# A mixture of experts: the 32 spare rows of each expert taken four experts at a time

## The chip, the cores and the metric

One core of a Trainium2 chip runs the whole program. The metric is the time of one execution on the device, in microseconds. Each kernel is run several times and the median counts.

## The reference

Four blocks in a row on 4096 tokens of 256 features, in fp32: attention, a local-attention transformer, a state-space scan, and a mixture of experts. The change lies in the last one. It has 32 experts; each token goes to the expert with the highest probability, and an expert takes at most 160 tokens (C below), the first ones in token order:

```python
C = int(math.ceil(CAPACITY_FACTOR * T / E))
...
g = jnp.einsum('ech,ehf->ecf', buf, w_gate)
u = jnp.einsum('ech,ehf->ecf', buf, w_up)
y = jnp.einsum('ecf,efh->ech', jax.nn.silu(g) * u, w_down)
out_tok = y.reshape(E * C, H)[jnp.clip(slot, 0, E * C - 1)]
out_tok = jnp.where(accepted[:, None], out_tok * gate[:, None], 0.0)
return (xt + out_tok).reshape(B, S, H)
```

T is 4096, E is 32, so C is 160: a tile of 128 rows and 32 spare rows. Feature sizes H and F are 256 each.

## The kernel before

Each block is one or two phases that follow one another; nothing of a phase overlaps the next, apart from early loads. The last, phase_moe, has two parts. In the first, eight chunks of 512 tokens are projected, normalised and routed; GpSimd scatters each token's row (its normalised features, its residual sum, its gate and its number: 514 fp32 words) to its expert's slot in a table in HBM, slots_x.

In the second part, here called the expert stage, the experts are taken in order, and each engine runs its own list of steps; they meet by semaphores:

- SP: load_weights(e) loads the three 256x256 matrices of expert e into a ring of RING buffers, and waits for the down products of the expert that had the buffer.
- ScalarE: load_rows(e) loads the expert's 160 rows from slots_x as two transfers (128 rows, L2852, and 32 rows, L2853). Six experts are loaded ahead of the loop; in the loop ScalarE computes the silu of expert e (L2880) and then issues the rows of expert e + 6.
- TensorE, in each turn e of its loop: expand(e), the gate and up products with the weights stationary and all 160 rows moving (L2945); turn_rows(e + 2), the transposes of the rows, for each half of the features one of 128 rows (L2932) and one of 32 (L2933); and reduce(e - 1), the down products with the rows stationary, once for 128 rows and once for 32 (L2956).
- VectorE: multiply (L2794, silu times up), put_xeT (L2786, the transposed rows out of PSUM), put_y (L2803, gate times product plus residual sum, once for 128 rows and once for 32) and tokens (L2813, the rows' numbers as integers).
- GpSimd: two indirect scatters per expert into the output (L2701).

PSUM tiles of the stage (p_x, p_g, p_u, p_y) have two buffers each, xeT and hidden two, y four and xe eight.

## Time and profile before

| what | us |
|---|---|
| median of three runs | 3643.21 |
| lowest and highest | 3635.83, 3643.5 |
| span of the profiled execution, first to last instruction | 3631.7 |

The profile is of one execution. It records the span; what lies around the span is not in it, and no time of that execution other than the span is given. All positions below are microseconds from the start of the span. Engines: PE is TensorE (PEld its weight loads), DVE is VectorE, ACT is ScalarE, POOL is GpSimd; a q behind the name is the engine's queue of DMA issues. L2945 is line 2945 of the kernel. A row of the timeline gathers neighbouring instructions of a kind: start, length, count (x8); PE's ends are modelled and overlap the next start, so a pace is read from one start to the next. An fp32 product is recorded as two instructions, a transpose as one.

### The profile page before, as it was taken

How to read it: one execution, taken by the hardware profiler on the slowest of the kernel's cores; microseconds unless marked ns; L12 is line 12 of the kernel's file. 1: busy time of each engine (PE TensorE's matmuls, PEld its weight loads, DVE VectorE, ACT ScalarE, POOL GpSimd, SP SyncE). 2: the span in 40 equal slices, each digit the busy share in tenths (PEclk: the TensorE clock that was granted, in tenths of full speed). 3: DMA queues.
4: the chain of work that ended last, by engine and by line, in shares of the span. 5: the costliest groups of instructions: out<-in, count | busy, mean ns of one | idle time of the engine just before them, and what ended most of it. 6: DMA issues, size and time to landing. Idle time of an engine off the chain costs nothing. (4 is left out here: it accounts for less than half of the span.)

```text
span 3631.7 us, 52306 instructions
## 1 busy us (share of the span) xinstructions
PE 3234.2 (89%) x18096; PEld 1975.7 (54%) x18096; DVE 2456.1 (68%) x4653; ACT 1848.7 (51%) x3942; POOL 1431.3 (39%) x992
## 2 busy tenths in 40 slices
PE   8599999979999799999999899897388888887798
PEld 5244444346666555566666555332255565555676
DVE  8488887657777522377777232598599999996633
ACT  2177776836666411266666111366377777774100
POOL 4201111132222211132222111244699999995533
PEclk9699999989999899999999899998699999999899
DMA  5945676110020133000200221343615151512873
GB/s 169 161 62 88 78 99 123 28 38 23 23 65 23 51 133 96 22 23 25 67 23 17 69 69 39 101 159 130 240 59 204 58 204 59 203 58 98 296 226 117
DMA packets 276675, 347.29 MB, mean 96 GB/s; under 512 B 71168, under 2 KB 208368, under 8 KB 275772
## 3 DMA queue, kind: packets, MB, share of 16 engines
q1 hardware_dynamic: 261860, 308.29, 30.9%
q10 hardware_dynamic: 9432, 23.35, 1.9%
q0 software_dynamic: 5120, 12.30, 0.9%
q8 instruction: 145, 2.38, 0.3%
q14 instruction: 118, 0.97, 0.1%
HBM read 227.72 MB, written 112.80 MB: 94 GB/s over the span
## 5 line engine op out<-in xcount | busy, mean ns | idle before, releaser
L2373 POOL TENSOR_TENSOR H_feed<-H_ndu,H_bs 128x1024 f32<-128x1024 f32 x256 | 595.3, 2373 | 6.3 <-DMA H_bs<-between_bc 3.2
L888 ACT ACTIVATE B_probs<-B_p_exp,B_key_bias 128x512 f32<-128x512 f32 (+3 forms) x768 | 395.0, 582 | 162.6 <-PE B_p_exp L950 132.2
L779 DVE TENSOR_REDUCE B_part_max<-B_p_max 128x1 f32<-128x512 f32 (+3 forms) x768 | 374.5, 545 | 81.9 <-PE B_p_max L914 79.4
L1298 ACT ACTIVATE D_probs<-D_scores,D_neg,D_rq 128x256 f32<-128x256 f32 x512 | 283.1, 573 | 255.6 <-DVE D_neg L1219 255.6
L2344 ACT ACTIVATE H_decay<-H_ndt,H_rate 128x1024 f32<-128x1024 f32 x256 | 287.8, 1125 | 198.0 <-DVE H_turning L2426 103.2
L1658 PE MATMUL E_p_ag<-E_hT,FA_w 128*128 128x512 f32 x640 | 283.1, 602 | 1.9 <-ACT E_hT L1614 1.9
L911 PE MATMUL B_p_max<-B_k,B_q 100*128 100x512 bf16 (+3 forms) x768 | 256.9, 341 | 29.9 <-DMA B_q<-in_q_rows 20.0
L947 PE MATMUL B_p_exp<-B_q,B_k 100*128 100x512 bf16 (+3 forms) x768 | 250.6, 330 | 23.9 <-DMA B_q<-B_shift_rows 17.1
L2426 DVE TENSOR_TENSOR_SCAN H_turning<-H_decay,H_feed 128x1024 f32<-128x1024 f32 x112 | 253.5, 2274 | 24.1 <-POOL H_feed L2373 22.7
L2477 PEld LDWEIGHTS H_p_y<-H_minus,H_sT 128*128 128x128 f32 x1792 | 224.3, 199 | 76.2 <-ACT H_sT L2329 56.1
L2477 PE MATMUL H_p_y<-H_minus,H_sT 128*128 128x128 f32 x1792 | 232.6, 286 | 35.5 <-ACT H_sT L2329 35.5
L1156 POOL TENSOR_TENSOR D_rnorm<-D_norm,D_power 128x8 f32<-128x8 f32 x64 | 106.1, 1658 | 375.0 <-DVE D_norm L1174 375.0
L1630 ACT ACTIVATE E_gated<-E_p_ag,FA_b 128x512 f32<-128x512 f32 x96 | 62.6, 652 | 372.9 <-PE E_p_ag L1658 353.7
L2329 ACT ACTIVATE H_sT<-H_p_T,H_cT 128x128 f32<-128x128 f32 x896 | 242.9, 387 | 11.7 <-PE H_p_T L2467 11.4
L1353 PE MATMUL D_p_qk<-LA_wqkv,D_hT 128*128 128x512 f32 x512 | 242.3, 617 | 0.9 <-ACT D_hT L1273 0.9
L1216 DVE CUSTOM_DVE_ANT_0 D_scores<-D_scores,D_mask 128x256 f32<-128x256 f32 x512 | 201.9, 457 | 55.0 <-PE D_scores L1380 54.8
L2426 DVE TENSOR_TENSOR_SCAN H_decay<-H_decay,H_feed 128x1024 f32<-128x1024 f32 x96 | 218.9, 2280 | 15.5 <-POOL H_feed L2373 15.5
L1160 POOL TENSOR_TENSOR D_rnorm<-D_norm,D_power 128x8 f32<-128x8 f32 x64 | 106.7, 1667 | 287.7 <-DVE D_norm L1174 287.7
L1658 PEld LDWEIGHTS E_p_ag<-E_hT,FA_w 128*128 128x128 f32 x640 | 121.9, 192 | 155.3 <-issue 151.6
L1585 DVE SCALAR_TENSOR_TENSOR E_act_out<-E_p_ag,FA_b,E_gated 128x512 f32<-128x512 f32 x96 | 67.8, 706 | 198.7 <-ACT E_gated L1630 198.7
L2485 PE MATMUL H_p_y<-H_part,H_minus 128*128 128x512 f32 x384 | 184.5, 603 | 9.6 <-DVE H_part L2402 9.5
L911 PEld LDWEIGHTS B_p_max<-B_k,B_q 100*128 100x128 bf16 x768 | 75.3, 98 | 208.2 <-DVE B_part_max L779 131.4
(269 smaller groups left out, 6858.2 us busy)
## 6 DMA issues: line engine op xcount, KB each, us to landing
H_bs<-between_bc SPq DMA_DIRECT2D x64, 512.0 KB, 8.0
H_cs<-between_bc SPq DMA_DIRECT2D x36, 512.0 KB, 8.5
B_q<-between_q_parts SPq DMA_DIRECT2D x90, 128.0 KB
B_k<-between_k_parts SPq DMA_DIRECT2D x90, 128.0 KB
between_slots_x<-E_clear ACTq DMA_DIRECT2D x4, 2570.0 KB, 18.8
I_xe<-between_slots_x ACTq DMA_DIRECT2D x32, 257.0 KB, 3.9
LA_base<-between_z SPq DMA_DIRECT2D x64, 128.0 KB, 2.2
between_z<-D_z SPq DMA_DIRECT2D x64, 128.0 KB, 1.7
```

Of the source, the lines that this page charges most:

```text
L779: nc.vector.reduce_max(part_max[:, g % 2, kc, qb, h:h + 1], p_max[:, use % 3, 0:keys], AX.X).then_inc(maxed, 1)
L888: nc.scalar.activation(probs[:, x % PROBS, skip:512], p_exp[:, n % SCORES, skip:512], ACT.Exp, bias=key_bias[:, g % SETS, kb - 4 * Q + 4, ...
L911: last = nc.tensor.matmul(p_max[:, use % 3, 0:keys], q[0:KR, u, h, qb * P:(qb + 1) * P], k[0:KR, u, h, 512 * kc:512 * kc + keys], start=Tr ...
L947: last = nc.tensor.matmul(p_exp[:, n % SCORES, skip:512], k[0:KR, u, h, kb * P:(kb + 1) * P], q[0:KR, u, h, 512 * Q + skip:512 * Q + 512], ...
L1298: last = nc.scalar.activation(probs[:, place[m], :, :].rearrange("p a b -> p (a b)"), scores[:, place[m], :, :].rearrange("p a b -> p (a b ...
L1353: last = nc.tensor.matmul(p_qk[:, m, :], hT[:, i % 2, k, :], wqkv[:, k, m * INNER:(m + 1) * INNER], start=k == 0, stop=k == KD - 1)
L1658: last = nc.tensor.matmul(p_ag[:, m % 2, n, :], w1[:, k, at:at + P], hT[:, i % 2, k, :], **flags)
L2329: last = nc.scalar.activation(sT[:, k % 2, h * HB + b, :], p_T[:, h, b, :], ACT.Copy, scale=cT[:, i % 2, h * HB + b, s:s + 1])
L2344: nc.scalar.activation(decay[:, n % 2, :], ndt[:, g % 2, :], ACT.Exp, scale=rate[:, m, s:s + 1]).then_inc(decayed, 1)
L2373: nc.gpsimd.tensor_tensor(feed[:, n % AHEAD, :], ndu[:, g % 2, :], bs[:, s, :], ALU.mult).then_inc(fed, 1)
L2426: nc.vector.tensor_tensor_scan(out, decay[:, n % 2, :], feed[:, n % AHEAD, :], 0.0, ALU.mult, ALU.add).then_inc(scanned, 1)
L2477: last = nc.tensor.matmul(p_y[:, h, b * P:(b + 1) * P], sT[:, k % 2, h * HB + b, :], minus[:, :], start=False, stop=False)
```

## The change

The expert stage treats the spare rows of four experts, a quad, as one tile of 128 rows.

- ScalarE loads an expert's 128 rows as one transfer, and the 32 spare rows of each expert of a quad into a quarter of the partitions of a tile xr, of which there are two (load_rests: four transfers). The first quad's are issued before all other rows, the second's after the first six experts' rows, and quad f + 1's in turn 4f + 1, behind the row load of that turn.
- TensorE turns the spare rows of a quad with two transposes of 128 rows, at the head of turn_rows of the quad's first expert. expand is as before, on 160 columns. reduce has only the 128 rows. Behind the reduce of a quad's last expert, reduce_rests computes the down products of the four experts' spare rows, each expert in its own strip of 32 columns of the array and its own 32 partitions of one PSUM tile.
- VectorE copies the turned spare rows once per quad and evacuates their products once per quad; GpSimd scatters them once per quad.
- xeT and hidden have eight buffers, and the ring of weights has twelve. A weight buffer is free when reduce_rests of its quad is done. p_y's two buffers are used in turn by reduce and reduce_rests.

The core of the diff:

```diff
-        K, XB, RING, XE, YR = CHUNKS, 4, 10, 8, 4
+        K, XB, RING, XE, YR = CHUNKS, 4, 12, 8, 4
+        QUAD, HR = 4, 8
+        QUADS = EXPERTS // QUAD
...
-        token_int = a.sb("token_int", [P, XE, 2, 1], I32)
+        token_int = a.sb("token_int", [P, XE, 1], I32)
+        token_rest = a.sb("token_rest", [P, 2, 1], I32)
...
-        xe = a.sb("xe", [P, XE, 2, ROW])
-        xeT = a.sb("xeT", [P, 2, KD, CAPACITY])
+        xe = a.sb("xe", [P, XE, ROW])
+        xr = a.sb("xr", [P, 2, ROW])
+        xeT = a.sb("xeT", [P, HR, KD, CAPACITY])
         sg = a.sb("sg", [P, 2, KD, CAPACITY])
-        hidden = a.sb("hidden", [P, 2, KD, CAPACITY])
-        y = a.sb("y", [P, YR, 2, DIM])
+        hidden = a.sb("hidden", [P, HR, KD, CAPACITY])
+        y = a.sb("y", [P, YR, DIM])
+        y_rest = a.sb("y_rest", [P, 2, DIM])
...
-        p_x = bank[:, 0:2, 0:KD * CAPACITY]
+        p_x = bank[:, 0:2, 0:KD * P]
+        p_xr = bank[:, 0, KD * P:2 * KD * P].rearrange("p (k j n) -> p k j n", k=KD, j=QUAD)
         p_g = bank[:, 2:4, 0:KD * CAPACITY]
         p_u = bank[:, 4:6, 0:KD * CAPACITY]
-        p_y = bank[:, 6:8, :].rearrange("p u (s d) -> p u s d", s=2)
+        p_y = bank[:, 6:8, 0:DIM]
...
+        def y_use(e):
+
+            return e + e // QUAD
+
+        def rest_use(f):
+            return f * (QUAD + 1) + QUAD
...
             def load_weights(e):
                 r = e % RING
-                reached(sp, down, e - RING + 1)
+                if e >= RING:
+                    sp.wait_ge(down, e - RING + 1)
+                    sp.wait_ge(rest_down, (e - RING) // QUAD + 1)
                 for dst, name in ((wg, "w_gate"), (wu, "w_up"), (wd, "w_down")):
...
             for e in range(EXPERTS):
-                pool.wait_ge(y_ready, e + 1)
+                pool.wait_ge(y_ready, y_use(e) + 1)
                 pool.wait_ge(tokens_ready, e + 1)
-                for t, rows in enumerate((P, REST)):
-                    pool.indirect_dma_start(T["out"][:, :], bass.IndirectOffsetOnAxis(token_int[0:rows, e % XE, t, :], axis=0),
-                                            y[0:rows, e % YR, t, :], None, bounds_check=TOKENS - 1, oob_is_err=False
-                                            ).then_inc(returned[e % YR], 16)
+                pool.indirect_dma_start(T["out"][:, :], bass.IndirectOffsetOnAxis(token_int[:, e % XE, :], axis=0),
+                                        y[:, e % YR, :], None, bounds_check=TOKENS - 1, oob_is_err=False
+                                        ).then_inc(returned[e % YR], 16)
+                if e % QUAD == QUAD - 1:
+                    f = e // QUAD
+                    pool.wait_ge(y_ready, rest_use(f) + 1)
+                    pool.wait_ge(rest_tokens_ready, f + 1)
+                    pool.indirect_dma_start(T["out"][:, :], bass.IndirectOffsetOnAxis(token_rest[:, f % 2, :], axis=0),
+                                            y_rest[:, f % 2, :], None, bounds_check=TOKENS - 1, oob_is_err=False
+                                            ).then_inc(rest_returned[f % 2], 16)
...
             def put_xeT(e):
                 dve.wait_ge(xe_turned, e + 1)
-                reached(dve, gate_up, 2 * (e - 1))
-                nc.vector.tensor_copy(xeT[:, e % 2, :, :].rearrange("p k n -> p (k n)"), p_x[:, e % 2, :]
+                reached(dve, gate_up, 2 * (e - HR + QUAD if e % QUAD == 0 else e - HR + 1))
+                if e % QUAD == 0:
+                    own = slice(e % HR, e % HR + QUAD)
+                    nc.vector.tensor_copy(xeT[:, own, :, P:CAPACITY], p_xr.rearrange("p k j n -> p j k n"))
+                nc.vector.tensor_copy(xeT[:, e % HR, :, 0:P], p_x[:, e % 2, :].rearrange("p (k n) -> p k n", k=KD)
                                       ).then_inc(xeT_ready, 1)
 
             def multiply(e):
                 u = e % 2
                 dve.wait_ge(silu, e + 1)
                 dve.wait_ge(gate_up, 2 * e + 2)
-                reached(dve, down, e - 1)
-                nc.vector.tensor_tensor(hidden[:, u, :, :].rearrange("p k n -> p (k n)"),
+                if e >= HR:
+                    dve.wait_ge(down, e - HR + 1)
+                    dve.wait_ge(rest_down, (e - HR) // QUAD + 1)
+                nc.vector.tensor_tensor(hidden[:, e % HR, :, :].rearrange("p k n -> p (k n)"),
                                         sg[:, u, :, :].rearrange("p k n -> p (k n)"), p_u[:, u, :], ALU.mult
                                         ).then_inc(hidden_ready, 1)
 
...
+                reached(dve, returned[b], 16 * (e // YR))
+                nc.vector.scalar_tensor_tensor(y[:, b, :], p_y[:, y_use(e) % 2, :], xe[:, x, GATE:GATE + 1], xe[:, x, SUM],
+                                               ALU.mult, ALU.add).then_inc(y_ready, 1)
+
+            def put_y_rest(f):
+                dve.wait_ge(rest_down, f + 1)
+                reached(dve, rest_returned[f % 2], 16 * (f // 2))
+                nc.vector.scalar_tensor_tensor(y_rest[:, f % 2, :], p_y[:, rest_use(f) % 2, :], xr[:, f % 2, GATE:GATE + 1],
+                                               xr[:, f % 2, SUM], ALU.mult, ALU.add).then_inc(y_ready, 1)
...
                     put_xeT(e + 2)
                 if e:
                     put_y(e - 1)
+                    if e % QUAD == 0:
+                        put_y_rest(e // QUAD - 1)
                 tokens(e)
+                if e % QUAD == 1:
+                    tokens_rest(e // QUAD)
             put_y(EXPERTS - 1)
+            put_y_rest(QUADS - 1)
...
             def load_rows(e):
                 b, at = e % XE, e * CAPACITY
                 reached(act, xe_turned, e - XE + 1)
-                reached(act, y_ready, e - XE + 1)
+                if e >= XE:
+                    act.wait_ge(y_ready, y_use(e - XE) + 1)
                 reached(act, tokens_ready, e - XE + 1)
-                act.dma_start(xe[:, b, 0, :], T["slots_x"][at:at + P, :]).then_inc(xe_loaded[b], 16)
-                act.dma_start(xe[0:REST, b, 1, :], T["slots_x"][at + P:at + CAPACITY, :]).then_inc(xe_loaded[b], 16)
+                act.dma_start(xe[:, b, :], T["slots_x"][at:at + P, :]).then_inc(xe_loaded[b], 16)
+
+            def load_rests(f):
+                if f >= 2:
+                    act.wait_ge(xe_turned, (f - 2) * QUAD + 1)
+                    act.wait_ge(y_ready, rest_use(f - 2) + 1)
+                    act.wait_ge(rest_tokens_ready, f - 1)
+                for j in range(QUAD):
+                    at = (f * QUAD + j) * CAPACITY + P
+                    act.dma_start(xr[REST * j:REST * j + REST, f % 2, :], T["slots_x"][at:at + REST, :]
+                                  ).then_inc(xr_loaded[f % 2], 16)
...
+            load_rests(0)
             for e in range(XE - 2):
                 load_rows(e)
+            load_rests(1)
...
                 if e + XE - 2 < EXPERTS:
                     load_rows(e + XE - 2)
+                if e % QUAD == 1 and QUAD <= e < EXPERTS - QUAD:
+                    load_rests(e // QUAD + 1)
...
             def turn_rows(e):
-                b, u = e % XE, e % 2
-                pe.wait_ge(xe_loaded[b], 32 * (e // XE + 1))
+                b, u, f = e % XE, e % 2, e // QUAD
+                pe.wait_ge(xe_loaded[b], 16 * (e // XE + 1))
                 reached(pe, xeT_ready, e - 1)
+                if e % QUAD == 0:
+                    pe.wait_ge(xr_loaded[f % 2], 16 * QUAD * (f // 2 + 1))
+                    for k in range(KD):
+                        nc.tensor.transpose(p_xr[:, k, :, :].rearrange("p j n -> p (j n)"),
+                                            xr[:, f % 2, k * P:(k + 1) * P], ident[:, :])
                 for k in range(KD):
-                    cols = slice(k * P, (k + 1) * P)
-                    at = k * CAPACITY
-                    nc.tensor.transpose(p_x[:, u, at:at + P], xe[:, b, 0, cols], ident[:, :])
-                    last = nc.tensor.transpose(p_x[:, u, at + P:at + CAPACITY], xe[0:REST, b, 1, cols],
-                                               ident[0:REST, 0:REST])
+                    last = nc.tensor.transpose(p_x[:, u, k * P:(k + 1) * P], xe[:, b, k * P:(k + 1) * P], ident[:, :])
                 last.then_inc(xe_turned, 1)
...
+                                                    ww[:, r, k, m * P:(m + 1) * P], xeT[:, e % HR, k, :],
...
             def reduce(e):
-                r, u = e % RING, e % 2
+                r, u = e % RING, y_use(e) % 2
                 pe.wait_ge(hidden_ready, e + 1)
-                reached(pe, y_ready, e - 1)
-                for t, rows in enumerate((P, REST)):
-                    for k in range(KD):
-                        last = nc.tensor.matmul(p_y[0:rows, u, t, :], hidden[:, u, k, t * P:t * P + rows],
-                                                wd[:, r, k, :], start=k == 0, stop=k == KD - 1)
+                reached(pe, y_ready, y_use(e) - 1)
+                for k in range(KD):
+                    last = nc.tensor.matmul(p_y[:, u, :], hidden[:, e % HR, k, 0:P], wd[:, r, k, :],
+                                            start=k == 0, stop=k == KD - 1)
                 last.then_inc(down, 1)
+
+            def reduce_rests(f):
+                u = rest_use(f) % 2
+                pe.wait_ge(y_ready, rest_use(f) - 1)
+                for k in range(KD):
+                    for j in range(QUAD):
+                        e = f * QUAD + j
+                        last = nc.tensor.matmul(p_y[REST * j:REST * j + REST, u, :], hidden[:, e % HR, k, P:CAPACITY],
+                                                wd[:, e % RING, k, :], start=k == 0, stop=k == KD - 1,
+                                                tile_position=(0, REST * j))
+                last.then_inc(rest_down, 1)
...
                 if e:
                     reduce(e - 1)
+                    if e % QUAD == 0:
+                        reduce_rests(e // QUAD - 1)
             reduce(EXPERTS - 1)
+            reduce_rests(QUADS - 1)
```

Two places of the program, as the engines' lists have them. TensorE before, one turn of the loop: down products, expand, four transposes, down products of the next:

```order
L2956 MATMUL I_bank<-I_wd,I_hidden 128x256 x2
L2956 MATMUL I_bank<-I_wd,I_hidden 32x256 x2
L2945 MATMUL I_bank<-I_xeT,I_wg 128x160 x4
L2945 MATMUL I_bank<-I_xeT,I_wu 128x160 x4
L2932 MATMUL I_bank<-I_ident,I_xe 128x128
L2933 MATMUL I_bank<-I_ident,I_xe 128x32
L2932 MATMUL I_bank<-I_ident,I_xe 128x128
L2933 MATMUL I_bank<-I_ident,I_xe 128x32
```

TensorE of the change, from the end of turn 4 through turn 5 to the transposes of turn 6 (L3014 is reduce, L3024 reduce_rests, L3004 expand, L2990 and L2993 turn_rows):

```order
L3014 MATMUL I_bank<-I_wd,I_hidden 128x256 x2
L3024 MATMUL I_bank<-I_wd,I_hidden 32x256 x8
L3004 MATMUL I_bank<-I_xeT,I_wg 128x160 x4
L3004 MATMUL I_bank<-I_xeT,I_wu 128x160 x4
L2993 MATMUL I_bank<-I_ident,I_xe 128x128 x2
L3014 MATMUL I_bank<-I_wd,I_hidden 128x256 x2
L3004 MATMUL I_bank<-I_xeT,I_wg 128x160 x4
L3004 MATMUL I_bank<-I_xeT,I_wu 128x160 x4
L2990 MATMUL I_bank<-I_ident,I_xr 128x128 x2
L2993 MATMUL I_bank<-I_ident,I_xe 128x128 x2
```

The 32-row products have left reduce and stand once per quad, and the quad's transposes (of xr) stand one turn behind the turn in which ScalarE issues their loads, as the next lists show. ScalarE before, one turn (silu, two row loads) and the head of the next:

```order
L2880 ACTIVATE I_sg<-I_bank 128x320
L2852 DMA I_xe<-between_slots_x 128x514
L2853 DMA I_xe<-between_slots_x 32x514
L2880 ACTIVATE I_sg<-I_bank 128x320
L2852 DMA I_xe<-between_slots_x 128x514
```

ScalarE of the change, turns 4, 5 and 6 (L2936 is the silu, L2897 load_rows, L2906 load_rests):

```order
L2936 ACTIVATE I_sg<-I_bank 128x320
L2897 DMA I_xe<-between_slots_x 128x514
L2936 ACTIVATE I_sg<-I_bank 128x320
L2897 DMA I_xe<-between_slots_x 128x514
L2906 DMA I_xr<-between_slots_x 32x514 x4
L2936 ACTIVATE I_sg<-I_bank 128x320
```

The second transfer of each expert has gone, and in turn 5 four stand between its row load and the silu of turn 6.

## Rows read from the trace of the kernel before

**Rows 1.** The page's head: length of the profiled execution.

```profile
span 3631.7 us, 52306 instructions
```

**Rows 2.** Chain that ended last, 3400 to 3632 us: shares, then start, length.

```profile
by line: PE I_bank L2945 33.5%; PE I_bank L2956 28.0%; PE I_bank L2932 5.1%; PE I_bank L2933 4.7%; PE I_bank L2892 4.7%; POOL between_slots_x L2679 4.3%; issue 4.2%; DMA between_slots_x<-I_row,I_slot_int 2.5%; DMA I_xe<-between_slots_x 1.7%
...
3403.82 0.87 PE I_bank L2901 x8
3407.76 7.00 PE I_bank L2892 x32
...
3440.14 5.91 DMA between_slots_x<-I_row,I_slot_int
...
3447.48 4.06 DMA I_xe<-between_slots_x
...
3452.95 4.21 PE I_bank L2945 x16
```

**Rows 3.** Timeline of TensorE, one expert: start, length, engine, line, what.

```profile
3534.76 1.35 PE L2945 MATMUL I_bank<-I_xeT,I_wg 128*128 128x160 f32 x8
...
3537.04 0.27 PE L2932 MATMUL I_bank<-I_ident,I_xe 128*128 128x128 f32 x1
...
3537.85 2.11 PE L2956 MATMUL I_bank<-I_wd,I_hidden 128*128 128x256 f32 x8
3539.89 1.35 PE L2945 MATMUL I_bank<-I_xeT,I_wg 128*128 128x160 f32 x8
```

**Rows 4.** Timeline of TensorE, the last experts.

```profile
3611.98 1.25 PE L2945 MATMUL I_bank<-I_xeT,I_wu 128*128 128x160 f32 x8
3613.07 1.03 PE L2956 MATMUL I_bank<-I_wd,I_hidden 128*128 128x256 f32 x4
```

**Rows 5.** Timeline of TensorE, attention and feed-forward: products in column strips.

```profile
427.10 0.64 PE L965 MATMUL B_p_acc<-B_probs,B_v 128*32 128x256 f32 x8
427.68 0.28 PE L911 MATMUL B_p_max<-B_k,B_q 100*128 100x256 bf16 x1
...
1284.46 1.95 PE L1663 MATMUL E_p_ag<-E_hT,FA_w 128*64 128x256 f32 x16
1286.34 1.09 PE L1644 MATMUL E_p_T<-FA_ident,E_hn 128*128 128x128 f32 x8
```

**Rows 6.** Timeline of all engines: SP's and ScalarE's DMA issues in one expert.

```profile
3534.86 0.37 SPq L2638 DMA_DIRECT2D I_wg<-in_w_gate  x1
...
3536.15 0.44 ACT L2880 ACTIVATE I_sg<-I_bank 128x320 f32<-128x320 f32 x1 [4.69 <-PE I_bank L2945]
3536.23 0.33 ACTq L2852 DMA_DIRECT2D I_xe<-between_slots_x  x1
...
3536.59 0.45 ACTq L2853 DMA_DIRECT2D I_xe<-between_slots_x  x1
```

**Rows 7.** DMA issues, 3480 to 3560 us: count, KB, median us to landing.

```profile
I_xe<-between_slots_x ACTq DMA_DIRECT2D x16, 257.0 KB, 3.9
...
I_xe<-between_slots_x ACTq DMA_DIRECT2D x16, 64.2 KB, 4.8
```

**Rows 8.** DMA issues, 3426 to 3440 us, the burst before the stage.

```profile
I_wd<-in_w_down SPq DMA_DIRECT2D x4, 256.0 KB, 7.7
...
between_slots_x<-I_row,I_slot_int POOLq DMA_INDIRECT x7, 6.3
```

**Rows 9.** Timeline of TensorE behind a gap (in brackets, with its releaser).

```profile
2472.12 1.13 PE L2131 MATMUL F_p_dt<-F_low,F_w_dt 16*128 16x512 f32 x4 [2.22 <-ACT F_low L2012]
```

**Rows 10.** Windows: length, PE, PEld, DVE, ACT, POOL busy; PEclk, DMA, GB/s.

```profile
2474.00:2477.00 3.00, 3.00 (x5) 1.13 (x4) 3.00 (x2) 2.03 (x4) 2.67 (x1) 0.50 0.01 1
...
3472.00:3552.00 80.00, 80.00 (x439) 58.10 (x438) 30.45 (x94) 7.00 (x16) 28.03 (x32) 1.00 0.79 242
```

**Rows 11.** Timeline of all engines at the end.

```profile
3617.16 0.86 DVE L2803 SCALAR_TENSOR_TENSOR I_y<-I_bank,I_xe 128x256 f32<-128x256 f32 x2 [1.06 <-PE I_bank L2956]
...
3620.54 0.88 POOL L2701 DMA_INDIRECT out_x<-I_y,I_token_int  x1 [0.30 <-issue]
```

More of the change, by code:

```diff
@@ L2604, in phase_moe @@
         xe_loaded = [a.sem(f"xe_loaded_{b}") for b in range(XE)]
+        xr_loaded = [a.sem(f"xr_loaded_{b}") for b in range(2)]
         xe_turned = a.sem("xe_turned")
@@ L2610, in phase_moe @@
         down = a.sem("down")
+        rest_down = a.sem("rest_down")
         y_ready = a.sem("y_ready")
@@ L2613, in phase_moe @@
         tokens_ready = a.sem("tokens_ready")
+        rest_tokens_ready = a.sem("rest_tokens_ready")
         returned = [a.sem(f"returned_{b}") for b in range(YR)]
+        rest_returned = [a.sem(f"rest_returned_{b}") for b in range(2)]
         block = ctx.enter_context(nc.Block())
@@ L2697, in _ @@
             for e in range(EXPERTS):
-                pool.wait_ge(y_ready, e + 1)
+                pool.wait_ge(y_ready, y_use(e) + 1)
                 pool.wait_ge(tokens_ready, e + 1)
-                for t, rows in enumerate((P, REST)):
-                    pool.indirect_dma_start(T["out"][:, :], bass.IndirectOffsetOnAxis(token_int[0:rows, e % XE, t, :], axis=0),
-                                            y[0:rows, e % YR, t, :], None, bounds_check=TOKENS - 1, oob_is_err=False
-                                            ).then_inc(returned[e % YR], 16)
+                pool.indirect_dma_start(T["out"][:, :], bass.IndirectOffsetOnAxis(token_int[:, e % XE, :], axis=0),
[8 more added lines that the diff above has]
+                                            ).then_inc(rest_returned[f % 2], 16)
             for b in range(YR):
-                pool.wait_ge(returned[b], 32 * EXPERTS // YR)
+                pool.wait_ge(returned[b], 16 * EXPERTS // YR)
+            for b in range(2):
+                pool.wait_ge(rest_returned[b], 16 * QUADS // 2)
         @block.vector
@@ L2798, in put_y @@
             def put_y(e):
-                u, b, x = e % 2, e % YR, e % XE
+                b, x = e % YR, e % XE
                 dve.wait_ge(down, e + 1)
-                reached(dve, returned[b], 32 * (e // YR))
-                for t, rows in enumerate((P, REST)):
-                    last = nc.vector.scalar_tensor_tensor(y[0:rows, b, t, :], p_y[0:rows, u, t, :],
-                                                          xe[0:rows, x, t, GATE:GATE + 1], xe[0:rows, x, t, SUM],
-                                                          ALU.mult, ALU.add)
@@ L2806, in put_y @@
-                last.then_inc(y_ready, 1)
+                reached(dve, returned[b], 16 * (e // YR))
[6 more added lines that the diff above has]
+                                               xr[:, f % 2, SUM], ALU.mult, ALU.add).then_inc(y_ready, 1)
@@ L2808, in tokens @@
             def tokens(e):
                 x = e % XE
-                dve.wait_ge(xe_loaded[x], 32 * (e // XE + 1))
-                reached(dve, returned[e % YR], 32 * (e // YR))
-                for t, rows in enumerate((P, REST)):
-                    last = nc.vector.tensor_scalar(token_int[0:rows, x, t, :], xe[0:rows, x, t, TOKEN:TOKEN + 1],
-                                                   -1.0, float(TOKENS), ALU.mult, ALU.add)
-                last.then_inc(tokens_ready, 1)
+                dve.wait_ge(xe_loaded[x], 16 * (e // XE + 1))
@@ new lines, in tokens, with tokens_rest @@
+                reached(dve, returned[e % YR], 16 * (e // YR))
+                nc.vector.tensor_scalar(token_int[:, x, :], xe[:, x, TOKEN:TOKEN + 1], -1.0, float(TOKENS), ALU.mult, ALU.add
+                                        ).then_inc(tokens_ready, 1)
+            def tokens_rest(f):
+                dve.wait_ge(xr_loaded[f % 2], 16 * QUAD * (f // 2 + 1))
+                reached(dve, rest_returned[f % 2], 16 * (f // 2))
+                nc.vector.tensor_scalar(token_rest[:, f % 2, :], xr[:, f % 2, TOKEN:TOKEN + 1], -1.0, float(TOKENS),
+                                        ALU.mult, ALU.add).then_inc(rest_tokens_ready, 1)
@@ L2945, in expand @@
                             last = nc.tensor.matmul(p[:, u, m * CAPACITY:(m + 1) * CAPACITY],
-                                                    ww[:, r, k, m * P:(m + 1) * P], xeT[:, u, k, :],
+                                                    ww[:, r, k, m * P:(m + 1) * P], xeT[:, e % HR, k, :],
                                                     start=k == 0, stop=k == KD - 1)
```

1 line of the change is left out of this document (removed).

## The prediction

> **What bounds the kernel now.** I read the page's head first, then the chain that ended last, then the timelines of the stage that the diff touches. The program is 3631.7 us long [rows 1]; the median of the runs, 3643.2 us, is 11.5 us above that, and I take this part as unchanged. The diff touches only the expert stage, the last 180 us. In its stretch of the chain the reader is to see that nearly everything is TensorE: 33.5% expand (L2945), 28.0% down products (L2956), 9.8% the rows' transposes (L2932, L2933) [rows 2]. From 3472 to 3552 us TensorE is busy for 80.00 us of 80.00 at a granted clock of 1.00, VectorE for 30.45, GpSimd for 28.03, ScalarE for 7.00, and the DMA engines for a share of 0.79 [rows 10]. So each microsecond taken off TensorE here counts, until something now hidden comes out. One expert reads, in the timeline: expand 3534.76 to 3537.04 (2.28 us), turn_rows to 3537.85 (0.81), reduce to 3539.89 (2.04): 5.13 us [rows 3].
>
> **The change on TensorE, step by step.** In the profile an fp32 product is two records, a transpose one.
> *Transposes.* Four become two. The 32-row ones change the array's shape and cost far more than their size: four take 0.81 us, while eight transposes of 128 rows in a row take 0.87, so 0.109 each [rows 2, 3]. Two are 0.22 us; 0.59 less for 30 experts (two are turned before the first expand) is -17.7 us. Seven quads get two more, +1.5 us (the first quad's lie in the start, below).
> *Down products of the 128 rows.* Four records instead of eight. 32 records of that shape take 7.00 us, 0.219 each [rows 2]: 0.88 us instead of 2.04, for 32 experts -37.1 us.
> *Expand.* Same work. Its last eight records take 1.09 us (3611.98 to 3613.07), 0.136 each [rows 4]; sixteen would be 2.18, and 2.28 is paid because it follows a product of another shape. Only the eight experts behind a reduce_rests still follow one: 24 x 0.10 = -2.4 us.
> *Spare rows' products.* Per quad 16 records of 32 columns in four strips. Do strips run side by side? The attention has this shape: eight records, four strips, 256 wide, from 427.10 to 427.68, 0.58 us [rows 5]; two rounds of 0.219 are 0.44, and 0.14 is the change of shape. Two strips agree: 16 records in 1.88 us, 1284.46 to 1286.34 [rows 5], where one after another they would need 3.5. Four rounds and 0.14 are 1.02 us a quad: +8.2 us.
> TensorE's sum is -17.7 + 1.5 - 37.1 - 2.4 + 8.2 = **-47.5 us**. An expert falls to 3.28 us, a quad to 14.5 (3.6 an expert).
>
> **What is late next: the load of the spare rows.** ScalarE issues load_rests(f + 1) in turn 4f + 1, and turn_rows of the quad's first expert comes in turn 4f + 2, one turn later; before, every row was loaded six experts ahead. Count from the start of expand in turn 5. ScalarE issues its row load 1.47 us in (3536.23 against 3534.76) and a second one from 1.83 [rows 3, 6]; that slot and the three after it are now the four spare-row loads, up to 0.45 us long with 0.03 between them [rows 6], so the fourth starts at 3.27. TensorE ends turn 5 at 2.28 + 0.22 + 0.88 = 3.38 and is at turn_rows(8) at 5.56. The wait is landing time less 2.3 us. A 64 KB row load lands 4.8 us after its issue in the steady stage [rows 7]: **2.5 us**, with reduce and the next expand queued behind it. It happens for quads 2 to 7, six times: +15.0 us. The bounds: the 256 KB load issued ahead of it lands in 3.9 us [rows 7] and has no queue of its own before it, and a spare-row load has only 64 KB, so even no wait is possible; above, at the moment of these loads SP has just been released for twelve weight loads in one go, and in such a burst before the stage the transfers land in 6.3 us (rows scattered by GpSimd) and 7.7 us (w_down) [rows 8], waits of 4.0 and 5.4. I take 4.8, the same transfer in the same stage.
> The Trainium skill, page "DMA: Bandwidth & Descriptors", section on the anatomy of one DMA, gives about 2.0 us plus bytes over 436 GB/s, 2.2 us for 64 KB, for the GpSimd path. By it the load would be there at 5.4, before TensorE, and the sum would be the one without a wait; the trace's 4.8 us says otherwise.
>
> *Clock.* Behind a TensorE gap of 2.22 us [rows 9] the stretch 2474 to 2477 ran at 0.50, 1.2 GHz, 3.00 us of it [rows 10]: 1.5 us lost. The new waits are of that size; I charge it for half of them, +4.5 us, between 0 and +9.
>
> **The start.** Expand(0) begins at about 3452.9 [rows 2]. Four spare-row issues now stand ahead of the first expert's rows: its second expert's rows become the sixth issue instead of the third and fourth, about +1 us, given back by shorter cold transposes and taken again by a second copy on VectorE. Two more experts' weights (twelve buffers) are fetched while the last scatters land, where the last scatter took 5.91 us to land [rows 2]; in the burst before, scatters took 6.3 and the slowest weights 7.7 [rows 8]. I take +2.5, between +0.5 and +5.
>
> **The end.** From the last expert's first evacuation at 3617.16, three more issues of GpSimd ran, to 3621.42 [rows 11], 4.3 us. Now the last expert's scatter is issued during reduce_rests and put_y_rest, and one issue follows it: one evacuation instead of two (0.43) and, behind the rest of that scatter's issue, one more of at most 1 us; about 1.9 us, -2.4.
>
> **Costed at nothing.** VectorE loses two of its six instructions per expert (a second evacuation, a second token row) and gains three per quad; at today's 1.95 us an expert (30.45 of 80.00, over 5.13) it would be half busy in 3.6 us even if it lost none, and its copies feed an expand two turns later. GpSimd's issues fall from 8 to 5 a quad. The weights are hidden by the ring: at share 0.79 and 5.13 us an expert needs 4.05 us of all DMA engines, four of them 16.2. They are released in quads, those of 12 to 15 at turn 5, 7 x 3.6 = 25 us before use, a lead of 9 us. A quad without waits lasts 14.5, so the lead shrinks by 1.7 us a quad, over four quads by 6.8: still enough. Without that cover it would be up to 7 us.
>
> **Sum:** -47.5 + 15.0 + 4.5 + 2.5 - 2.4 = -27.9 us; span 3631.7 - 27.9 = 3603.8, time 3643.2 - 27.9 = **3615 us**.
>
> **The rivals.**
> *No wait (0.20).* For it: the loads are small, and in the burst the scatters, issued after the last weights, land sooner than these (6.3 against 7.7 us) [rows 8]. Against: 4.8 us. Sum -47.5 + 2.5 - 2.4 = -47.4: 3596 us.
> *A longer wait (0.14).* Landing 6.3 to 7.7 us: waits of 4.0 to 5.4, six times 24 to 32 us, and the clock each time, +9: 3629 to 3637 us. For it: the release of twelve weight loads just ahead. Against: one 64 KB piece, not 256 KB.
> *Strips one after another (0.04), the change not doing what it says.* At reduce's present pace, 2.04 us for 8 records, 16 of them take 4.1 us a quad instead of 1.02, +24.6 us: 3640. Against: the 0.58 us of rows 5.
> *Weights late (0.03).* +7 us on 3615: 3622.
> *Slower (0.03).* The same wait, decided by its landing time alone: with the clock lost each time (+9), six waits must exceed (47.4 + 7.3 - 9) / 6 = 7.6 us, so a spare-row load must land later than 9.9 us after issue. That is beyond the 7.7 of rows 8, at twice the steady value. At 12 us: 3643.2 - 47.4 + 9 + 58 = 3663.
> My forecast, a wait of 1 to 4 us, has 0.56.
>
> **How the numbers follow.** The predicted time is the forecast's, 3615. Its own range with the bounds of wait, clock and start is 3601 to 3629. The whole range takes in the case without a wait and the nearer half of the longer wait: 3596 to 3631. Three runs of this kernel lie 7.7 us apart, so 0.2%, 7.3 us, is about what a measurement can tell. Faster by more: no wait, forecast, late weights and most of the longer wait, 0.91. Within: the rest of that and the serial strips, 0.06. Slower: 0.03.
>
> **What the profile after would show.** Right: turns of 3.3 us (two transposes 0.22, four down records 0.88); reduce_rests 16 records in 1.0 us; at turns 6, 10, ... 26 TensorE idle before the first spare-row transpose, released by the DMA into xr, about 2.5 us each; no idle before expand. Wrong: idle before expand, released by weights (the ring), by the copy of xeT (VectorE), or before reduce; sixteen strip records over 3 us; gaps of under 1 or over 4 us at the spare rows; a granted clock well under 1 through the stage. The 2.5 us rests on one landing time and is the number most likely to be off.

## The result, and the profile after

| | median us | lowest to highest | runs |
|---|---|---|---|
| before | 3639.72 | 3632.93 to 3643.5 | 6 |
| after | 3623.82 | 3620.21 to 3632.49 | 6 |

The ratio, as it is on record, is 0.9973, with a 95% interval of 0.9961 to 0.9984: of 3640 us that is 9.8 us less (5.8 to 14.2). The two medians of the table lie further apart, 15.9 us, and how the ratio was formed from the single times is not on record; the second occasion (after_again, below), with more runs, gives 11.6 us by its ratio and 13.0 by its medians. The forecast was 28 us less. The time of the median lies within the range, but the gain is between a third and little more than half of what was forecast.

The profiled execution of the changed kernel has a span of 3630.7 us and a time of 3632.49, the slowest of its six. Between the two lie 1.8 us, and 1.7 to 1.9 in every execution on record, so the prediction's "11.5 us around the span" was wrong: the profiled execution before must have taken about 3633.5 us, one of the faster ones, not a median one. The head of its page:

```profile
span 3630.7 us, 52188 instructions
```

Two spans should not be subtracted here. The first product of the last phase starts at 3342.5 us in this execution and at 3333.0 before, with the same code ahead of it. What compares is the expert stage itself, from the start of the first expand to the start of the last evacuation (VectorE's copy of a product out of PSUM), and its two ends:

| us | before | after |
|---|---|---|
| last scatter of the rows to the first expand | 12.7 | 14.9 |
| first expand to the start of the last evacuation | 164.7 | 151.7 |
| from there to the end of the span | 14.1 | 11.5 |

Together that is 13.4 us less.

The chain that ended last, after the change, over the first quad whose spare rows are loaded in the loop (start, length, what; x16 is the count of records):

```profile
3483.39 0.87 PE I_bank L3014 x4
3484.25 1.00 PE I_bank L3024 x16
3485.25 1.30 PE I_bank L3004 x8
3486.66 0.33 ACTq L2897
3487.10 0.40 ACTq L2906
3487.53 0.44 ACTq L2906
3488.00 0.44 ACTq L2906
3488.47 8.00 DMA I_xr<-between_slots_x
3496.61 0.66 PE I_bank L2990 x2
3497.27 0.43 PE I_bank L2993 x2
3497.70 1.71 PE I_bank L3014 x4
3499.41 2.53 PE I_bank L3004 x16
3502.16 0.86 PE I_bank L3014 x4
3503.02 2.17 PE I_bank L3004 x16
```

L3004 is expand, L3014 reduce, L3024 reduce_rests, L2990 the spare rows' transposes, L2993 those of the 128 rows, L2906 load_rests. Every TensorE part has the predicted size: reduce 0.87 us (predicted 0.88, before 2.04 [rows 3]), the sixteen strip records 1.00 (1.02), expand 2.17 (2.18). But at the head of quad 2 the chain leaves TensorE and runs through the last of the four spare-row loads, 8.00 us from its issue to its landing. The waits say the same in one row (what was waited for, us in all, times, longest):

```profile
PE I_bank L2990 <- DMA I_xr<-between_slots_x: 25.0, 6, 5.7
```

The timeline of TensorE shows the gap, and what is slow behind it (the bracket is the idle time ahead and its releaser):

```profile
3488.55 1.25 PE L3004 MATMUL I_bank<-I_xeT,I_wg 128*128 128x160 f32 x8
3489.63 1.25 PE L3004 MATMUL I_bank<-I_xeT,I_wu 128*128 128x160 f32 x8
3496.61 0.66 PE L2990 MATMUL I_bank<-I_ident,I_xr 128*128 128x128 f32 x2 [5.73 <-DMA I_xr<-between_slots_x]
3497.06 0.64 PE L2993 MATMUL I_bank<-I_ident,I_xe 128*128 128x128 f32 x2
3497.49 1.92 PE L3014 MATMUL I_bank<-I_wd,I_hidden 128*128 128x256 f32 x4
```

The gaps at quads 2 to 7 are 5.73, 5.03, 4.83, 4.37, 4.87 and 0.17 us. Four rows of windows: the stretch that holds the gap, the last part of that gap, the work behind it, and a stretch clear of any gap (length, PE busy, PEld, DVE, ACT, POOL, granted clock, DMA share, GB/s):

```profile
3490.90:3496.60 5.70, 0.00 (x0) 0.02 (x1) 0.49 (x1) 0.00 (x0) 0.11 (x1) 0.70 1.08 290
3493.20:3496.60 3.40, 0.00 (x0) 0.02 (x1) 0.00 (x0) 0.00 (x0) 0.00 (x0) 0.50 1.09 295
3496.60:3500.40 3.80, 3.79 (x14) 3.44 (x15) 1.30 (x4) 0.00 (x0) 0.00 (x0) 0.55 1.01 329
3500.50:3507.00 6.50, 6.50 (x55) 5.64 (x53) 2.67 (x7) 0.87 (x2) 1.97 (x2) 1.00 0.48 122
```

The granted clock falls to 0.50, 1.2 GHz, while TensorE still waits, and stays there for the first work behind the wait: reduce takes 1.71 us instead of 0.87. It happened behind each of the five long gaps: 3.4, 6.0, 4.1, 3.4 and 2.8 us of TensorE's work ran at 0.50, 19.7 in all, which took 9.8 us longer than at 1.00. In the gap the DMA engines are full (share 1.08); in the clear stretch they are half busy (0.48). What fills them is issued at the same moment. SP's and ScalarE's issues (start, length):

```profile
3485.37 0.37 SPq L2657 DMA_DIRECT2D I_wg<-in_w_gate  x1
...
3488.44 0.44 SPq L2657 DMA_DIRECT2D I_wg<-in_w_gate  x1
3488.93 1.02 SPq L2657 DMA_DIRECT2D I_wu<-in_w_up  x1
...
3493.76 0.83 SPq L2657 DMA_DIRECT2D I_wd<-in_w_down  x1
```
```profile
3487.10 2.37 ACTq L2906 DMA_DIRECT2D I_xr<-between_slots_x  x4
```

SP issues twelve weight loads from 3485.37 on, released by the end of the quad's reduce_rests, and the four spare-row loads stand from 3487.10 in the middle of them. The landing times over the stage (issues, KB each, median us):

```profile
I_xe<-between_slots_x ACTq DMA_DIRECT2D x26, 257.0 KB, 2.8
I_wg<-in_w_gate SPq DMA_DIRECT2D x20, 256.0 KB, 7.9
I_wu<-in_w_up SPq DMA_DIRECT2D x20, 256.0 KB, 8.0
I_wd<-in_w_down SPq DMA_DIRECT2D x20, 256.0 KB, 8.6
```

The last spare-row load of each quad appears in the chain: 8.00, 6.38, 6.24, 6.59, 7.17 and 2.43 us. The sixth is the last quad's, when no weights are left to load; a row load of 257 KB stands ahead of it on ScalarE's queue as it does for the others:

```profile
3575.18 7.17 DMA I_xr<-between_slots_x
...
3596.10 2.43 DMA I_xr<-between_slots_x
```

### The profile page after: what moved, and what is told of

It is laid out like the page before. It is cut to its first block and busy times, and to the rows that moved or that the text cites. A ratio compares the mean times of both kernels' runs of the same rounds, so it can differ in the third digit from the quotient of the medians.

```text
span 3630.7 us, 52188 instructions
## 1 busy us (share of the span) xinstructions
PE 3202.5 (88%) x18048; PEld 1973.5 (54%) x18048; DVE 2445.3 (67%) x4613; ACT 1847.3 (51%) x3942; POOL 1410.3 (39%) x968
## 5 line engine op out<-in xcount | busy, mean ns | idle before, releaser
L2329 ACT ACTIVATE H_sT<-H_p_T,H_cT 128x128 f32<-128x128 f32 x896 | 242.3, 387 | 13.9 <-PE H_p_T L2467 13.6
```

The lines of the kernel that those rows point to most:

```text
L2329: last = nc.scalar.activation(sT[:, k % 2, h * HB + b, :], p_T[:, h, b, :], ACT.Copy, scale=cT[:, i % 2, h * HB + b, s:s + 1])
```

## The experiments

**Theory:** the spare-row loads are issued too late and land late because they share the DMA engines with the twelve weight loads; the waits and the clock behind them take back some 34 of TensorE's 47.5 us. **Rivals:** the loads are slow because they are four small ones; the 47.5 us were never there in full; what was lost lies in the ring or at the start. Every ratio is to runs of the kernel before on the same chip in the same session. "Stage" is from the start of the first expand to the start of the last evacuation, in the one profiled execution of a run, 164.68 us before.

**The changed kernel again (after_again), no edit.**

> The changed kernel as it is, beside the others on one chip. Theory (the spare rows' loads land late and TensorE waits for them): six waits at the spare-row transposes, 25 us in sum, of which the last, without weight loads beside it, under 1.5 us; expand(0) to the last reduce_rests about 152 us; 10 to 16 us faster than before. Rival (what is missing was lost ahead of the expert stage: the last two chunks of the routing stood 12.2 and 12.6 us apart in the profile of the change, 10.9 in that of before): the same two gaps again, and shorter waits in the expert stage.

Ratio 0.9968 (0.9958 to 0.9978), medians 3621.70 and 3634.68 us. Stage 151.09 us, five gaps of 4.82, 5.33, 4.49, 4.36 and 5.50, 24.5 us in all; the sixth, of the last quad, was not there. The rival fell: the last two chunks of the routing, 12.2 and 12.6 us apart in the first profile after the change, are 10.9 apart here, as before. The result and its cause repeat.

**A third buffer for the spare rows (early_rests).** Their loads are issued a quad earlier, so the landing time no longer matters. All indices of xr follow the third buffer.

```diff
-        QUAD, HR = 4, 8
+        QUAD, HR, XR = 4, 8, 3
...
-        xr = a.sb("xr", [P, 2, ROW])
+        xr = a.sb("xr", [P, XR, ROW])
...
-            load_rests(1)
+            for f in range(1, XR):
+                load_rests(f)
...
-                if e % QUAD == 1 and QUAD <= e < EXPERTS - QUAD:
-                    load_rests(e // QUAD + 1)
+                if e % QUAD == 1 and QUAD <= e and e // QUAD + XR - 1 < QUADS:
+                    load_rests(e // QUAD + XR - 1)
```

> A third buffer for the spare rows, so that a quad's loads are issued one quad (four turns) earlier. Theory: the six waits (25 us) and the turns at half clock behind them (about 10 us) go, expand(0) to the last reduce_rests falls from 152 to about 117 us, and the kernel is about 35 us faster than the changed one, 45 to 50 faster than before. Rival (weights late: once TensorE runs unhindered, the four sets released at once don't arrive in time): idle before expand at the heads of quads, 2 us and more each, and a gain of 15 to 30 us only.

Ratio 0.9868 (0.9853 to 0.9882), median 3587.78 us: 48 us faster than before. Stage 117.13 us, 47.55 less than before. Windows of it, a long one, the densest part, and the stage's first microseconds:

```profile
3472.00:3552.00 80.00, 80.00 (x593) 72.55 (x592) 35.05 (x104) 9.70 (x23) 27.58 (x28) 1.00 0.99 316
3500.00:3540.00 40.00, 40.00 (x298) 36.27 (x297) 17.48 (x52) 4.82 (x11) 13.79 (x14) 1.00 1.07 345
3459.42:3463.64 4.22, 4.22 (x16) 4.22 (x17) 0.19 (x1) 1.72 (x2) 0.00 (x0) 0.50 0.80 185
```

The reader is to see 80.00 of 80.00 us of TensorE at a granted clock of 1.00, beside a DMA share of 0.99, against 0.79 in the same window before [rows 10]. In the chain the spare rows' transposes follow expand without a gap:

```profile
3481.83 2.17 PE I_bank L3005 x16
3484.00 0.22 PE I_bank L2991 x2
3484.22 0.22 PE I_bank L2994 x2
```

That the sum of -47.5 is met to a tenth is partly chance. The last row shows why: behind the wait for the first rows the stage starts at a granted clock of 0.50, and for how long differs between executions, 2.6 to 5.5 us in the five with a third buffer, whose stages are 116.3 to 117.8 us long. With half of that time taken off, an estimate, all five are 115.0 us, and the two without quads 162.8 (3.8 and 2.9 us at 0.50): TensorE's sum is -47.8. So it was right, and what the changed kernel lost in its stage it lost to this wait and to the clock behind it.

**Weights behind the spare rows (weights_behind).** SP's first weight load of a quad waits until the spare rows have landed. Whether the weights cause the long landing is asked here directly.

```diff
                     sp.wait_ge(rest_down, (e - RING) // QUAD + 1)
+                    if e % QUAD == 0:
+                        sp.wait_ge(xr_loaded[(e // QUAD - 1) % 2], 16 * QUAD * ((e // QUAD - 1) // 2 + 1))
```

> SP issues the first of the twelve weight loads of a quad only when the spare rows that ScalarE issues in the same turn have landed. Theory (the burst of weight loads beside them makes them late): landing falls from 6.2 to 8.0 us to about 3, the first five waits from 4.4 to 5.7 us each to about 1, the clock stays at 1.00, and the kernel is about 25 to 30 us faster than the changed one. Rival (they are simply issued too late, four issues one behind another, whatever runs beside them): waits of 3 us and more remain and the gain is under 12 us.

Ratio 0.9923 (0.9908 to 0.9937), median 3604.32 us, stage 131.98 us: between theory and rival. The first burst shows the theory pure: the last spare-row load is issued at 3480.44, and SP, which waits for its landing, goes on 2.3 us later; TensorE has no gap at this quad.

```profile
3479.09 1.79 ACTq L2908 DMA_DIRECT2D I_xr<-between_slots_x  x4
```
```profile
3482.76 0.37 SPq L2659 DMA_DIRECT2D I_wg<-in_w_gate  x1
...
3489.45 0.94 SPq L2659 DMA_DIRECT2D I_wd<-in_w_down  x1
3500.51 0.37 SPq L2659 DMA_DIRECT2D I_wg<-in_w_gate  x1
```

But that burst now ends at 3489.45 (its last issue), and its 256 KB loads are still under way when the next spare rows are issued, from 3493.67 on, the last at 3495.04. What SP's queue (q1) and ScalarE's (q10) moved from 3495 to 3496 (packets, MB, share of the 16 DMA engines' time):

```profile
q1 hardware_dynamic: 341, 0.33, 103.2%
q10 hardware_dynamic: 2, 0.00, 1.1%
```

The weights had the engines to themselves, and the spare rows moved only after them: the last landed 5.4 us after its issue. Four quads waited, 3.12, 3.87, 3.37 and 1.22 us, 11.6 in all. The expected clock of 1.00 did not hold throughout either: behind the gaps of 3.87 and 3.37 us it fell to 0.50 for 3.4 us each. The weights in flight are the cause whether they are issued at the same moment or a little ahead.

**One load for the quad (one_load).** The four loads of 64 KB become one of 256 KB whose outermost dimension is the four experts; the waits count 16 for a quad.

```diff
-                for j in range(QUAD):
-                    at = (f * QUAD + j) * CAPACITY + P
-                    act.dma_start(xr[REST * j:REST * j + REST, f % 2, :], T["slots_x"][at:at + REST, :]
-                                  ).then_inc(xr_loaded[f % 2], 16)
+                at = f * QUAD * CAPACITY
+                act.dma_start(xr[:, f % 2, :], T["slots_x"][at:at + QUAD * CAPACITY, :].rearrange(
+                    "(j c) d -> j c d", c=CAPACITY)[:, P:CAPACITY, :]).then_inc(xr_loaded[f % 2], 16)
```

> The four spare-row loads of a quad as one transfer of 256 KB. Theory (the engines' queues are full of weights, the data are late): the issue starts 1.4 us earlier than the fourth did, but the bytes and the burst are the same, so the waits fall by 0.5 to 1.5 us each and the kernel gains 3 to 10 us. Rival (the four issues, stretched by SP's issues beside them to 0.7 and 1.4 us, are what costs): the waits fall by 2.5 us and more each, and 20 us are gained.

Ratio 1.0016 (1.0007 to 1.0026), median 3639.62 us: the whole gain is gone, and it went against both theories. Stage 165.01 us, gaps of 7.01, 6.26, 6.89, 7.52, 7.70 and 1.57, 36.9 us in all. The first and the last of its loads in the chain:

```profile
3479.66 10.66 DMA I_xr<-between_slots_x
...
3598.18 5.22 DMA I_xr<-between_slots_x
```

The last has no weights beside it and still takes 5.22 us, where the last of four small ones took 2.43 and a row load of the same 257 KB takes 2.8. So it is the form of this transfer, not its size or the load on the engines, that makes it slow. While it moves, from 3600.60 to 3602.60, ScalarE's queue keeps this much of the 16 engines busy:

```profile
q10 hardware_dynamic: 90, 0.18, 25.4%
```

That is the time of four engines, 4.1 of 16; the small loads of the changed kernel held 60.9% from 3596.70 to 3597.40. The Trainium skill, page "DMA: Bandwidth & Descriptors", section "Why a DMA increments its semaphore by 16 and not by 1", says that the number of DMA engines used is the largest up to 16 that divides the slowest dimension of both sides (other than 1). For the merged load this gives 4 (four experts on the side of HBM), for a load of 32 or 128 rows 16. The trace agrees, with its 25.4%.

**A busy wait (busy_wait).** Before each of the five long waits TensorE does 32 transposes whose result is overwritten. The wait is as long, but the idle part of it is short: this asks what the clock costs.

```diff
+                    if 2 * QUAD <= e < EXPERTS - QUAD:
+                        for n in range(32):
+                            nc.tensor.transpose(p_xr[:, n % KD, :, :].rearrange("p j n -> p (j n)"), ident[:, :], ident[:, :])
                     pe.wait_ge(xr_loaded[f % 2], 16 * QUAD * (f // 2 + 1))
```

> The changed kernel, with 32 extra transposes of a constant tile (3.5 us at 0.109 each) on TensorE ahead of the five waits of 4.4 to 5.7 us; their results are overwritten. Theory (each of these waits also costs TensorE's clock, 3.4 to 6.8 us at 0.50 each): the idle before the spare-row transposes shrinks to under 2 us, no stretch of 0.50 stands in the expert stage, and expand(0) to the last reduce_rests falls from 151 to about 143 us, though more is computed: 5 to 9 us faster than the changed kernel. Rival (the slow turn behind a wait comes from the gap itself, not from the clock): still 151 us or more.

Ratio 0.9951 (0.9937 to 0.9965), median 3617.05 us. Stage 143.95 us, against 151.1 and 151.7. The quad that waits second:

```profile
3505.18 3.66 PE L2990 MATMUL I_bank<-I_ident 128*128 128x128 f32 x32
3509.47 0.44 PE L2993 MATMUL I_bank<-I_ident,I_xr 128*128 128x128 f32 x2 [0.63 <-DMA I_xr<-between_slots_x]
3509.97 1.03 PE L3017 MATMUL I_bank<-I_wd,I_hidden 128*128 128x256 f32 x4
```

Useless work made the stage 7 to 8 us faster. On the whole kernel's time this is only just visible: 0.9951 against 0.9968 and 0.9973, on another chip, with intervals that overlap. Gaps and transposes together are 7.8 + 5 x 3.66 = 26.1 us, no less than the 24.5 and 25.0 of the idle waits; what is gone is the low clock. One stretch of 3.4 us at 0.50 was left, against five, of 3.4 to 6.8 us. By difference the clock costs the changed kernel 151.7 - 117.1 - 25.0 = 9.6 us, near the 9.8 counted from its work at 0.50. The one stretch left here costs 1.7 us by the same count. So the expectation of no such stretch did not quite hold, but the loss does come from the clock and not from the gap itself.

**The ring of twelve alone (ring12_only).** The kernel before with `RING` 12 instead of 10.

```diff
-        K, XB, RING, XE, YR = CHUNKS, 4, 10, 8, 4
+        K, XB, RING, XE, YR = CHUNKS, 4, 12, 8, 4
```

> The kernel before with twelve weight buffers and nothing else. Theory (two more experts' weights only delay the last scatters and the first rows): no difference in the expert stage, expand(0) 1 to 3 us later behind the last scatter than in the kernel before, which is 0.03 to 0.08% slower, not measurable. Rival (the ring gives something by itself): faster by over 2 us.

Ratio 1.0012 (1.0002 to 1.0021), medians 3638.51 and 3634.10 us; stage 164.24 us. Twelve buffers alone bring nothing, and may cost some microseconds: in the profiled executions 13.6 us instead of 12.7 pass between the last scatter and the first expand.

**Ten buffers with the early loads (early_ring10).** early_rests with `RING` 10.

```diff
-        K, XB, RING, XE, YR = CHUNKS, 4, 12, 8, 4
+        K, XB, RING, XE, YR = CHUNKS, 4, 10, 8, 4
```

> Spare rows one quad earlier, but ten weight buffers. Theory (the ring of twelve is what hides the weights once TensorE runs at 3.3 us a turn, since they are freed in quads): idle before expand for weights at several quads, 5 to 20 us in sum, and the kernel 5 to 20 us slower than with twelve. Rival (ten would have done): as fast as with twelve, a stage of 117 us without gaps.

Ratio 0.9859 (0.9844 to 0.9874), median 3582.96 us; stage 117.06 us without a gap. The theory that a release in quads needs twelve buffers fell.

**The first spare rows from SP (early_sp).** early_rests, with the loads of the first three quads' spare rows issued by SP, beside ScalarE's row loads, instead of by ScalarE ahead of and behind them.

```diff
+            for b in range(XB):
+                sp.wait_ge(scattered[b], 16 * CT * K // XB)
+            for f in range(XR):
+                for j in range(QUAD):
+                    at = (f * QUAD + j) * CAPACITY + P
+                    sp.dma_start(xr[REST * j:REST * j + REST, f % XR, :], T["slots_x"][at:at + REST, :]
+                                 ).then_inc(xr_loaded[f % XR], 16)
...
-            load_rests(0)
             for e in range(XE - 2):
                 load_rows(e)
-            for f in range(1, XR):
-                load_rests(f)
```

> As the kernel with a third spare-row buffer, with the first three quads' spare rows issued by SP, beside the first experts' rows from ScalarE, instead of four of them ahead of those and eight behind. Theory (four issues of 0.48 us stand ahead of the first rows): expand(0) comes 1.5 to 2 us sooner behind the last scatter, the stage stays at 117 us, the kernel 46 to 52 us faster than before. Rival (the transfers share the DMA engines, and what is issued sooner lands no sooner): expand(0) within 0.5 us of where it was.

Ratio 0.9872 (0.9857 to 0.9887), median 3589.72 us. Between the last scatter and the first expand 16.9 us pass, two more than in early_rests: the theory fell. In its chain the last of the first quad's spare-row loads, issued at 3455.58, takes 6.19 us to land, now that ScalarE's row loads run at the same time (no run separates them from SP's own eight further loads):

```profile
3455.58 6.19 DMA I_xr<-between_slots_x
```

**Twelve against ten on one chip (twelve, ten).** early_rests and early_ring10 again, side by side.

> Spare rows one quad earlier with twelve weight buffers, again, beside ten on one chip. Theory (two more experts' weights delay the scatters' landing and the first rows, and give nothing later): 14 to 15 us from the last scatter's issue to expand(0), a stage of 117 us without gaps. Rival (chance of one execution): under 13 us.

> The same with ten weight buffers. Theory: 12 to 13 us from the last scatter's issue to expand(0), a stage of 117 us without gaps, 1 to 4 us faster than with twelve. Rival (chance of one execution): no difference beyond 1 us, or gaps before expand in this execution.

Ratios 0.9858 (0.9841 to 0.9874) and 0.9871 (0.9855 to 0.9888), medians 3584.30 and 3589.12 us: no difference that these runs can measure, and the 1 to 4 us expected for ten did not show. In the chains one thing does differ each time, the landing of the last scatter of rows, first with twelve buffers, then with ten:

```profile
3445.07 7.22 DMA between_slots_x<-I_row,I_slot_int
```
```profile
3450.76 5.58 DMA between_slots_x<-I_row,I_slot_int
```

With twelve it lands 1.6 us later (in early_rests and early_ring10 6.75 and 5.43 us), as the prediction had argued from two more experts' weights on the same engines; from the last scatter to the first expand it is 14.7 and 14.1 us with twelve, 12.4 and 12.3 with ten. It is too little to show in the time.

## Why the prediction was wrong

*What bounds, and TensorE's sum: right.* The stage ran at TensorE's pace, and its difference was -47.55 us as measured (164.68 to 117.13) once the wait was gone, -47.8 with the clock at the stage's start allowed for. Each part has its predicted size, the four strips too (1.00 us for sixteen records). One slip in it is worth 0.1 us: seven expands follow a reduce_rests, not eight, since the last reduce_rests comes behind the last expand.

*The place of the wait: right.* In the turn ahead of quad 2 the fourth spare-row load was issued 3.22 us after the start of expand (3488.47 against 3485.25; predicted 3.27), and TensorE was ready for it 5.63 us after (predicted 5.56). There were six waits, the last of 0.17 us only, and no other new one of note. For quads 3 and 4 the place was off too: beside SP's burst the third of the four issues took 1.40 and 1.21 us, and the fourth came 0.9 and 0.8 us later than predicted. That is 1.7 us of the 25.0.

*The landing time: wrong. This is the step that failed.* I took 4.8 us, "the same transfer in the same stage" [rows 7], and with it waits of 2.5 us, +15.0 in all. It was 6.2 to 8.0 us for five quads and 2.43 for the sixth; the waits were 25.0 us, 10 more than the term. The row that I took was of an expert whose own three weight loads were its neighbours, while the change releases twelve at once. The text named that release and the burst before the stage in [rows 8], 6.3 to 7.7 us, as the upper bound; it was the nearest row by what stands beside the transfer, and that decides. weights_behind shows it: 2.3 us with no weights beside, 5.4 with the burst of the quad before. The outcome is the rival "a longer wait", which had 0.14: its 24 to 32 us of waits and 9 of clock are what came, 25.0 and 9.8.

*The clock: too small.* I charged half of six waits at 1.5 us, 4.5; it was all five long ones, 9.6 to 9.8 us, a little more than the upper bound of 9. The gap from which 1.5 us was read was 2.22 us long [rows 9, 10]; these were twice as long.

*Start and end: right.* +2.2 us in the profiled execution, +1.2 in the one of after_again (predicted +2.5), and -2.6 in both (-2.4).

*The weights' lead: harmless, though not for the reason given.* Waits kept the pace slow here. But with the third buffer and no waits TensorE stayed busy at a DMA share of 0.99, and with ten buffers too.

*The base: a slip.* The 11.5 us between the span and the median were not around the span but for the most part between two executions. It touches neither the forecast gain nor the 3615, which is the median of three less the gain; that median came down from 3643.2 to 3639.7 us with three more runs. The forecast's own range, 3601 to 3629, is not what its bounds add up to: with waits of 1 to 4 us and the bounds of clock and start it is 3600 to 3631. Nothing hangs on it.

Summed up, the terms as they came out are -47.5 + 25.0 + 9.6 + 2.2 - 2.6 = -13.3 us (13.4 by the table above). The 9.6 is what is left of the stage, so the sum closes by its making; the check on it is the 9.8 counted apart. The timed gain is 9.8 (5.8 to 14.2), and 11.6 (8.0 to 15.3) on the second occasion. The 2 to 4 us between the sum and these are within the intervals. One thing about them is open: the last phase starts at 3331.3 and 3333.0 us in the two profiled executions without quads and at 3332.6 to 3342.5 in ten with them, though the code ahead of it is the same. With one profiled execution of each kernel I can't tell a cost from scatter, and did not try to.

## What to carry to other kernels

A batched release makes a batched burst. When buffers come free four at a time, their loads go out together, and a small transfer issued in that moment lands at the burst's pace (here 6.2 to 8.0 us instead of 2.4); price it by a row from within a burst, not by the same transfer in the steady state. Whatever had a long lead before (here six experts) should keep one when it is regrouped: a third buffer of 128 rows was worth 36 us, three times the measured gain of the change without it. The version to use is the changed kernel with three spare-row buffers, at 0.9858 to 0.9871 of the time before, with ten or twelve weight buffers.

And before a span is set against a median, compare it with the time of its own execution.

## What was unexpected on the chip

- A transfer of 256 KB with four as its outermost dimension landed after 5.22 us with no weights beside it and 9.9 to 11.4 in the burst, where four transfers of 64 KB landed after 2.43 and 6.2 to 8.0, counted from the last issue. It kept four of the 16 DMA engines busy (25.4% of their time).
- Issues stretch in a burst. In the changed kernel a spare-row issue of ScalarE took 0.44 us and up to 1.40 beside SP's burst, one of SP's 0.47 at the head of the burst and up to 2.06 later. It isn't only two queues issuing at once: in weights_behind, with no spare rows beside them, the last three of SP's twelve took 0.90 to 0.96. What stretches them was not tested.
- Idle TensorE time costs twice: a wait of about 5 us lost a further 2 us to the clock (9.6 to 9.8 over five), and 32 useless transposes in each wait got 7 to 8 us of it back in the stage.
- A DMA share of 0.99 to 1.07 at 316 to 345 GB/s did not slow TensorE at all, with every load issued at least a quad ahead of its use.
